# Modulation rows on three engines, and a new order of the work ahead of the first scan, in a Mamba-style block with adaptive layer norm

## The reference

```python
mod = (silu(c) @ wmod).reshape(1, 6, 1, -1)          # c: 1 x 1024, wmod: 1024 x 6144
sa, ca, ga, sb, cb, gb = (mod[:, k] for k in range(6))
ga = (2 * (ga >= 0) - 1) * maximum(abs(ga), 0.25)     # gb alike
h = layernorm(x) * (1 + ca) + sa
x = x + ga * attn(h)
h = layernorm(x) * (1 + cb) + sb
x = x + gb * ffn(h)

def attn(x):                                          # state of 16 per channel
    xp = x @ x_proj_w.T                               # 32 of dt, 16 of B, 16 of C
    dt = softplus(xp[:, :32] @ dt_proj_w.T + dt_proj_b)
    h_t = exp(dt * A) * h_(t-1) + dt * B_t * x_t      # A = -exp(A_log), a scan over the tokens
    y_t = sum over states of h_t * C_t, + D * x_t

def ffn(x):                                           # 1024 -> 2752 -> 1024, each weight with a rank-16 addition
    return down(silu(gate(x)) * up(x))
```

## Time and profile before

| | us |
|---|---|
| median of three runs | 2287.67 (2287.53 to 2288.17) |
| the profiled execution | 2279.5 |
| its span, first to last instruction | 2277.7 |
| busy in the span: TensorE matmul / VectorE / ScalarE / GpSimd | 2044.7 / 1442.4 / 1041.2 / 1542.8 |

### The profile page before, as it was taken

One profiled execution on the slowest core, in us unless ns is written; L12 is line 12 of the kernel. 1 busy time (PEld: TensorE's weight loads), 2 busy tenths in 40 slices (PEclk: granted clock), 3 DMA queues, 4 the chain that ended last, 5 costly groups with the idle time before them and its releaser, 6 DMA issues.

```text
span 2277.7 us, 33011 instructions
## 1 busy us (share of the span) xinstructions
PE 2044.7 (90%) x11652; PEld 1860.5 (82%) x11652; DVE 1442.4 (63%) x2119; ACT 1041.2 (46%) x2330; POOL 1542.8 (68%) x960
## 2 busy tenths in 40 slices
PE   7587756878879989899999899999899999999999
PEld 4233235778869989799999799999799999999999
DVE  4665776778767878767778667778667774211111
ACT  3776765666554555444545344555343332210000
POOL 1578779998988877877867777867869895110100
PEclk9688877989989999999999999999999999999999
DMA  9799875778967768586768586768587877787786
GB/s 361 301 359 342 309 289 211 279 266 277 340 248 277 255 241 283 207 274 219 246 225 280 178 280 224 242 224 284 171 268 257 280 258 256 253 287 275 253 291 218
DMA packets 121204, 602.99 MB, mean 265 GB/s; under 512 B 10576, under 2 KB 23120, under 8 KB 80464
## 3 DMA queue, kind: packets, MB, share of 16 engines
q1 hardware_dynamic: 121040, 600.89, 75.0%
HBM read 514.63 MB, written 86.21 MB: 264 GB/s over the span
## 4 chain that ended last, share of the span: by engine, by line
PE 55%; DVE 13%; POOL 9%; ACT 8%; issue 7%; DMA 6%; DVEq 0%; SPq 0%; ACTq 0%; POOLq 0%
PE FP L780 48%; DVE ring L1186 5%; POOL ring L1300 4%; PE FP L663 4%; POOL y L1275 2%; DVE ring L1071 2%; DMA raw<-w_gu 2%; ACT SC L851 2%; DVE FP L1161 2%; DMA wts<-w_scratch 2%; PE FP L804 1%; POOL wts L1283 1%; ACT sqb L969 1%; PE FP L741 1%; DMA w_scratch<-wts 1%
## 5 line engine op out<-in xcount | busy, mean ns | idle before, releaser
L780 PE MATMUL FP<-xhi,wts 128*128 128x368 f32 (+2 forms) x4320 | 1078.4, 326 | 62.9 <-ACT dtb L974 29.6
L780 PEld LDWEIGHTS FP<-xhi,wts 128*128 128x128 f32 x4320 | 774.1, 194 | 73.2 <-issue 61.5
L1300 POOL TENSOR_TENSOR ring<-ring,c_row 128x736 f32<-128x736 f32 (+2 forms) x336 | 575.7, 1714 | 236.0 <-ACT hst L868 235.7
L780 PE MATMUL FP<-xlo,wts 128*128 128x368 f32 (+2 forms) x2160 | 700.3, 324 | 0.0
L851 ACT ACTIVATE SC<-dtb,aneg 128x368 f32<-128x368 f32 (+2 forms) x768 | 409.4, 538 | 592.9 <-DVE ring L1186 592.6
L780 PE MATMUL FP<-hhi,wts 128*128 128x368 f32 (+5 forms) x2376 | 571.1, 321 | 27.6 <-POOL hlo L1315 23.2
L1186 DVE TENSOR_TENSOR_SCAN ring<-SC,hst,ring 128x368 f32<-128x368 f32 (+1 forms) x640 | 579.3, 946 | 3.6 <-ACT SC L851 3.6
L1275 POOL TENSOR_TENSOR y<-y,ring 128x736 f32<-128x736 f32 (+1 forms) x320 | 554.7, 1733 | 13.9
L780 PEld LDWEIGHTS FP<-hhi,wts 128*128 128x128 f32 (+1 forms) x2376 | 406.7, 185 | 34.9 <-POOL hlo L1315 22.3
L780 PEld LDWEIGHTS FP<-xlo,wts 128*128 128x128 f32 x2160 | 418.8, 194 | 1.1
L780 PE MATMUL FP<-hlo,wts 128*128 128x368 f32 (+5 forms) x1188 | 379.4, 319 | 0.0
(11 more groups left out here) (104 smaller groups left out, 1929.7 us busy)
## 6 DMA issues: line engine op xcount, KB each, us to landing
wts<-w_scratch SPq DMA_DIRECT2D x249, 1152.0 KB, 5.3
wts<-w_scratch SPq DMA_DIRECT2D x91, 896.0 KB, 5.0
wts<-w_scratch SPq DMA_DIRECT2D x51, 1024.0 KB, 5.5
w_scratch<-wts SPq DMA_DIRECT2D x44, 1152.0 KB, 8.6
raw<-w_gu SPq DMA_DIRECT2D x44, 576.0 KB, 6.8
modw<-mod_w SPq DMA_DIRECT2D x24, 1024.0 KB, 10.4
w_scratch<-wts SPq DMA_DIRECT2D x16, 896.0 KB, 6.8
w_scratch<-wts SPq DMA_DIRECT2D x9, 1024.0 KB, 7.8
```

What stands on the lines that cost most here:

```text
L780: last = mm(out, w, x, start=(start and k == 0 and e == 0), stop=(stop and k == n - 1 and e == 2))
L1300: G.tensor_tensor(buf, buf, over_pair(c_of(k)), ALU.mult).then_inc(g_hc, 1)
```

## The change

The twelve blocks ahead of the first scan are shared by three engines. VectorE makes 0, 3, 5, 9 and 10 (before: 2, 4, 6, 9 and 11), GpSimd makes 1 and 4, TensorE the other five (before seven). GpSimd's way with a block is new, the item `grow`: it multiplies the whole block of 8 x 256 in place by silu(c), repeated along the columns, and then adds halves: 4 x 256, 2 x 256, 256. The subtraction in `consts` moves from VectorE to GpSimd. Only two preps instead of four stand ahead of the first scan; the other two are added to those spread over the groups. And the whole list ahead of the first scan is in a new order, so that each engine has its parts, and SyncE its loads, in a new order too. `mrow` has two slots instead of four.

```diff
--- before.py
+++ after.py
@@ -41,9 +41,10 @@
 MOD_BLOCKS = 6 * D // MOD_COLS
 MOD_SLOTS = 5
 MOD_EACH = D // MOD_COLS
-ROW_SLOTS = 4
-BY_VECTOR = [2, 4, 6, 9, 11]
-BY_TENSOR = [b for b in range(MOD_BLOCKS) if b not in BY_VECTOR]
+ROW_SLOTS = 2
+BY_VECTOR = [0, 3, 5, 9, 10]
+BY_GPSIMD = [1, 4]
+BY_TENSOR = [b for b in range(MOD_BLOCKS) if b not in BY_VECTOR + BY_GPSIMD]
 LATES = [range(MOD_EACH * n, MOD_EACH * (n + 1)) for n in range(3)] + [range(b, b + 1) for b in range(3 * MOD_EACH, MOD_BLOCKS)]
 
 
@@ -209,7 +210,7 @@
 OTF = [u for u in range(NU) if u % 3 == 1]
 PREP = [u for u in range(NU) if u not in OTF]
 NPREP = len(PREP)
-PREP_BEFORE = 4
+PREP_BEFORE = 2
 
 
 def first_pieces():
@@ -224,15 +225,18 @@
     def vrow(b):
         return [("vrow", b)] + ([("lmod", b + MOD_SLOTS)] if b + MOD_SLOTS < 3 * MOD_EACH else [])
 
+    def grow(b):
+        return [("grow", b)] + ([("lmod", b + MOD_SLOTS)] if b + MOD_SLOTS < 3 * MOD_EACH else [])
+
     def cen(k, c):
         return [("cen", k, c, q) for q in range(PAIRS)]
 
-    out = [("sum", 0, 0), ("sum2", 0, 0)] + row(0) + [("lprep",)] + cen(0, 0) + [("rowc", 0)] + row(1) + vrow(2) + [("rowc", 1)]
-    out += prep() + [("sq", 0, 0), ("sq2", 0, 0), ("consts",), ("col", 0), ("col", 1), ("col", 2)] + row(3) + vrow(4) + [("rowc", 3)]
-    out += prep() + [("rstd", 0, 0), ("col", 3)] + row(5) + [("rowc", 5)] + vrow(6) + [("late", 0), ("col", 4), ("col", 5)] + prep()
-    out += [("norm", 0, 0, q) for q in range(PAIRS)] + row(7) + [("rowc", 7), ("col", 6), ("col", 7), ("late", 1), ("mod", 0)] + row(8)
-    out += [("aff", 0, 0, q) for q in range(PAIRS)] + [("rowc", 8)] + vrow(9) + prep() + [("col", 8), ("proj", 0), ("col", 9)] + row(10)
-    out += [("xs", 0), ("lx", 1), ("rowc", 10), ("dt", 0, 0), ("dt", 0, 1)] + vrow(11) + [("sp", 0, 0), ("col", 10), ("col", 11), ("late", 2), ("mod", 1)]
+    out = vrow(0) + grow(1) + [("sum", 0, 0), ("sum2", 0, 0)] + cen(0, 0) + row(2) + [("rowc", 2), ("sq", 0, 0), ("sq2", 0, 0), ("lprep",)]
+    out += vrow(3) + grow(4) + [("col", 0), ("col", 1), ("col", 2)] + vrow(5) + [("rstd", 0, 0), ("consts",), ("col", 3), ("late", 0)]
+    out += row(6) + [("rowc", 6)] + [("norm", 0, 0, q) for q in range(PAIRS)] + prep() + [("col", 4), ("col", 5)] + row(7) + [("rowc", 7)]
+    out += [("col", 6), ("col", 7), ("late", 1), ("mod", 0)] + prep() + [("aff", 0, 0, q) for q in range(PAIRS)] + row(8) + [("rowc", 8)] + vrow(9) + vrow(10)
+    out += [("proj", 0), ("xs", 0), ("lx", 1), ("dt", 0, 0), ("dt", 0, 1)] + row(11) + [("rowc", 11), ("sp", 0, 0)]
+    out += [("col", 8), ("col", 9), ("col", 10), ("col", 11), ("late", 2), ("mod", 1)]
     out += [("ini", 0, 0), ("soft", 0, 0), ("sp", 0, 1), ("keep", 0, 0), ("soft", 0, 1), ("keep", 0, 1), ("first",)]
     a = MOD_EACH
     at = {}
...
@@ -397,7 +402,7 @@
         a_hi, a_ts, a_th, a_hh = sem("weight_hi_ready"), sem("lora_rounded"), sem("tanh_ready"), sem("hidden_hi_ready")
 
         v_const, v_c, v_mod, v_modstep, v_late = sem("vector_const_ready"), sem("silu_c"), sem("mod_ready"), sem("mod_step"), sem("mod_cols_copied")
-        v_acc = sem("mod_row_summed")
+        v_acc, g_acc, g_const = sem("mod_row_summed"), sem("mod_row_summed_by_gpsimd"), sem("dt_weights_low")
         v_cen, v_step, v_norm = sem("centered"), sem("rstd_step"), sem("normed")
         v_xs, v_soft, v_add, v_u = sem("xs_split"), sem("factor_used"), sem("dt_ready"), sem("u_ready")
         v_dbx, v_ev = sem("dbx_ready"), sem("y_evacuated")
...
@@ -648,12 +655,16 @@
                     bank_free(pe, "col", b)
                 if b in BY_VECTOR:
                     pe.wait_ge(v_acc, ND * (BY_VECTOR.index(b) + 1))
+                elif b in BY_GPSIMD:
+                    pe.wait_ge(g_acc, 4 * (BY_GPSIMD.index(b) + 1))
                 else:
                     pe.wait_ge(a_row, BY_TENSOR.index(b) + 1)
                 for i in range(MOD_COLS // P):
                     out = FP[:, bank, at + i:at + i + 1]
                     if b in BY_VECTOR:
                         last = mm(out, macc[:, BY_VECTOR.index(b) % 2, i * P:(i + 1) * P], ones[:, 0:1], start=True, stop=True)
+                    elif b in BY_GPSIMD:
+                        last = mm(out, gacc[:, BY_GPSIMD.index(b), i * P:(i + 1) * P], ones[:, 0:1], start=True, stop=True)
                     else:
                         last = mm(out, mrow[0:1, BY_TENSOR.index(b) % ROW_SLOTS, i * P:(i + 1) * P], ones[0:1, 0:1], start=True, stop=True)
                 last.then_inc(pe_col, 1)
@@ -735,7 +746,7 @@
                     if c == 0:
                         pe.wait_ge(d_const, N_CONST)
                         pe.wait_ge(a_const, 4)
-                        pe.wait_ge(v_const, 2)
+                        pe.wait_ge(g_const, 1)
                     bank_free(pe, *p)
                     for i in range(ND):
                         last = mm(bank_of(*p), xpw[:, i, :], tile_of(hb, c, i), start=(i == 0), stop=(i == ND - 1))
@@ -1087,6 +1098,7 @@
                 dve.wait_ge(v_late, (2, 3, len(LATES))[n])
                 if n == 0:
                     then(V.tensor_scalar(mod[:, CA, :], mod[:, CA, :], 1.0, None, ALU.add))
+                    dve.wait_ge(a_const, 2)
                     V.tensor_scalar(aneg[:, :], aneg[:, :], -1.0, None, ALU.mult).then_inc(v_mod, 1)
                 elif n == 1:
                     then(away_from_zero(mod[:, GA, :]))
@@ -1100,9 +1112,6 @@
                 kind = p[0]
                 if kind == "mod":
                     mod_vectors(p[1])
-                elif kind == "consts":
-                    dve.wait_ge(a_const, 3)
-                    V.tensor_tensor(dlo[:, :], dtw, dhi[:, :].bitcast(F32), ALU.subtract).then_inc(v_const, 1)
                 elif kind == "vrow":
                     b, i = p[1], BY_VECTOR.index(p[1])
                     acc = macc[:, i % 2, :]
@@ -1276,7 +1285,23 @@
 
             def piece(p):
                 kind = p[0]
-                if kind == "prep":
+                if kind == "consts":
+                    pool.wait_ge(a_const, 3)
+                    G.tensor_tensor(dlo[:, :], dtw, dhi[:, :].bitcast(F32), ALU.subtract).then_inc(g_const, 1)
+                elif kind == "grow":
+                    b, i = p[1], BY_GPSIMD.index(p[1])
+                    w = modw[:, b % MOD_SLOTS, :, :]
+                    pool.wait_ge(d_mod[b % MOD_SLOTS], (b // MOD_SLOTS + 1) * 16)
+                    if i == 0:
+                        pool.wait_ge(v_c, 2)
+                    G.tensor_tensor(w, w, vec[:, 3, :].unsqueeze(2).to_broadcast([P, ND, MOD_COLS]), ALU.mult).then_inc(g_acc, 1)
+                    pool.wait_ge(g_acc, 4 * i + 1)
+                    G.tensor_tensor(w[:, 0:4, :], w[:, 0:4, :], w[:, 4:8, :], ALU.add).then_inc(g_acc, 1)
+                    pool.wait_ge(g_acc, 4 * i + 2)
+                    G.tensor_tensor(w[:, 0:2, :], w[:, 0:2, :], w[:, 2:4, :], ALU.add).then_inc(g_acc, 1)
+                    pool.wait_ge(g_acc, 4 * i + 3)
+                    G.tensor_tensor(gacc[:, i, :], w[:, 0, :], w[:, 1, :], ALU.add).then_inc(g_acc, 1)
+                elif kind == "prep":
                     i = p[1]
                     s, w = i % PREP_SLOTS, lo_cols(PREP[i])
                     pool.wait_ge(a_prep, i + 1)
```

More of the change, by code:

```diff
@@ L368, in build @@
             macc = sb("macc", [P, 2, MOD_COLS], to=early)
+            gacc = sb("gacc", [P, 2, MOD_COLS], to=early)
         xhi = sb("xhi", [P, ND, TM], F32R)
@@ L474, in mod_used @@
                 engine.wait_ge(v_acc, ND * (BY_VECTOR.index(b) + 1))
+            elif b in BY_GPSIMD:
+                engine.wait_ge(g_acc, 4 * (BY_GPSIMD.index(b) + 1))
             else:
```

## The result

The changed kernel takes 2293.45 us (median of 20 runs) and the kernel before 2286.82 (20 runs): the ratio is 1.003, 95% interval 1.0021 to 1.0039, or +6.6 us. The change makes the kernel slower by 0.3%. A second set of runs gave 1.0033 (1.0019 to 1.0046).

What follows compares the result with a forecast made beforehand. The chain over VectorE bounds the work ahead of the first scan; only the first pass's instant can move. A start 4.4 later plus 5 for preparations gave +9.4: 2287.67 to 2297 us, range 2280 to 2304 for 8 in 10.

Steps and rivals of the forecast that it cites:

- The sum: Whole kernel: first scan 4.4 us later plus scan stage 5 us longer, +9.4 us, median 2297; chance 0.40.
- the start's term: Ahead of the first scan: it starts at 78.8 instead of 74.42, 4.4 us later.
- the stage's: From first scan to first feed-forward pass: 284 us plus 5 for the two moved preparations.
- the first rival: Scan stage: the DMA queue sets it, so the preparations cost 9.7 us; +14 in all, 2302; chance 0.12.
- third: Rival, scan stage: the moved preparations vanish in slack, leaving +4.4 us, 2292; chance 0.13.
- fourth: Rival, ahead of the scan: GpSimd's product goes at half price, start as before, +5 us, 2293; chance 0.08.
- The exclusion: Ahead of the scan: VectorE instructions with two SBUF inputs and GpSimd's exclude each other whole; accumulations take 1 to 5 us, not 0.485.
- Second rival: Ahead of the scan: VectorE and GpSimd run beside each other, scan near 65.1, 9.3 us earlier; 2283 or 2278; chance 0.22.
- A block on GpSimd: Ahead of the scan: product 4.52 us, sums 2.35, 1.26 and 0.72, together 8.85 us a block.
- The order ahead of the scan: Row 0 ends at 21.9, row 3 at 39.1, row 6 at 43.3, projection at 58.2; softplus's product at 69.1, not 64.73.
- The preparations: Scan stage: 46 instead of 44 weight preparations cost 4 to 5.3 us more by their chain shares, taken as 5.
- The table load: Softplus ahead of the scan: its 1.28 us load disappears, counted as nothing because another wait covers it.

Runs made afterwards that it cites:

- The sum in PSUM: Changed kernel with VectorE's running sum in PSUM instead of SBUF until the last of eight steps: 2284.78 us, ratio 1.0000 to the kernel before.
- The two kernels with doubled stores and splits: Kernel before with 11 of the 44 scan-stage preparations' weight stores made twice, ratio 1.0043, or their GpSimd splits done twice, ratio 1.0049.
- the remedy: VectorE's running sum in PSUM, here put into the kernel before with its old order and shares: 2282.27 us, ratio 0.9989.

## Why the prediction was right, step by step

- **The sum.** +9.4 forecast, +6.6 measured (4.8 to 8.9). The direction and the range held, and both mechanisms were there. But the start's term was too large by 2 to 4 us and the stage's too small by 2, and part of the closeness of the sum is luck: these two errors cancel in part. There is also a slip in the chances: all of the forecast and the first rival and half of the third and fourth make 0.625, not 0.57, so the chance of slower was written too low.
- **The exclusion** stood, for a step with two SBUF inputs, as a reading of one row, `dlo`. The changed trace has it in nine places (eight ahead of 36 us, one at 48.62): seven are accumulating steps with both inputs in SBUF, two are TENSOR_SCALAR with one. The sum in PSUM removes all of them. Second rival: its first half (steps keep 0.485) is wrong. Its start, 65.1 or 9.3 us earlier than in the kernel before, was nearly right for the kernel in which the exclusion is taken away (66.47, 7.9 earlier).
- **A block on GpSimd.** 8.85 forecast, 8.1 measured: the sums at 2.40, 1.32 and 0.79 close to the line's 2.35, 1.26 and 0.72, the product 3.60 and not 4.52.
- **The order ahead of the scan.** Row 0 ended at 21.9 as forecast (21.86 for centering's start), by luck: VectorE began 0.5 us later than forecast and had three steps left, not two, when GpSimd began, while GpSimd's product was 0.9 shorter. Row 3 ended at 35.1, not 39.1, for three reasons. The two products were 0.9 shorter each. Taking turns cost GpSimd 0.08 us between two instructions, where the forecast charged it 0.5 for a step of VectorE, so block 4's product began at 22.48 and not at 24.0. And between 30.8 and 32.4 GpSimd waited for ScalarE, so that VectorE made three steps freely. Row 6 began at 36.1 instead of 39.1, and then lost most of it, as TensorE ran it at the lower clock (below): it ended at 42.3, not 43.3. Columns 4 and 5 so came 1 us earlier than forecast, the projection ended at 56.5, not 58.2, and the product of softplus began at 67.03, not 69.1.
- **The first scan**, +4.4, is the term that was mis-sized: +1.6 and +0.7 in two profiles. Even that is not shown by them. The two kernels with doubled stores and splits have the start of the kernel before, and their first scans came at 76.40 and 77.03. In the second a row met a split (seven steps in 5.83 us instead of 3.61); in the first the rows were as before, and the projection took 5.41 us instead of 3.72, at a granted clock of 0.67. So a start moves by 2 us from execution to execution. The kernel before with two preparations taken out took 2292.63, the changed kernel on the same chip 2292.85: all that is left for the new order and shares is 0.2 us, give or take the two or three us of the intervals. I put the start's share at 0 to 2 us.
- **The preparations**, +5, measured 6.9 and 7.1. The shares of the chain underestimate: they charge a preparation only with its own stretches of the chain, while the doubled splits cost 0.44 of their length against the share's 0.2. The first rival (9.7 by the queue) overestimates: the queue's price is 0.8 us a MB, though the DMA engines are 91% busy from 80 to 320 us.
- **The table load** was saved on ScalarE and bought nothing for softplus's first product, as forecast: it followed the vectors of the gate (66.83 + 0.17, then 67.03). From there to the first scan it took 9.0 us and not the 9.7 of the forecast: VectorE's second softplus product no longer waited 0.62 us for ScalarE. Whether the table load did that is not shown.
- **What the forecast missed**: that the new order itself was good. With the exclusion gone, the new order and shares start the scan 6 to 8 us earlier than the kernel before (66.47 and 68.11 against 74.42), some 2 us of which the remedy gives the old order too (72.59). The exclusion and the moved preparations hid it.

## What to carry to other kernels

Before giving GpSimd a part of VectorE's work, count the SBUF inputs of what VectorE does at that time: with two of them VectorE and GpSimd took turns here, and a long instruction on GpSimd held up a short one, with everything queued behind it. A running sum in an idle bank of PSUM took VectorE out of this for almost nothing: 0.14 us more on the first step of a block. Work that "fits anywhere" has a price that depends on the stage: here moving a preparation from ahead of the scan into it cost 3.5 us net, though no engine is full there. Two of them were nearly free ahead of the scan in the old order (0.3 us), cost 1.6 us of the start in the new order with the sum in PSUM, and 3.0 to 3.9 where a split also met a row of VectorE. Doubling a part of the work in a few places measures such a price.

## What the runs showed of the hardware

- VectorE and GpSimd alternated, instruction by instruction, while both had work queued: a held step ended 0.28 to 0.29 us after GpSimd's instruction, and GpSimd's next began 0.08 us after its last. Which accumulating steps are held depends on their SBUF inputs: the same step with one input in PSUM took 0.487 to 0.490 beside GpSimd, and 0.84 to 3.89 with both in SBUF. The eighth step, with one SBUF input and its output in SBUF, took 0.481, also at 22.63 beside GpSimd's product. TENSOR_SCALAR differs: with one SBUF input and its output in SBUF it took 2.75 and 1.98 beside GpSimd (0.35 alone), while from SBUF to PSUM it took 0.49 at 41.10 with a split from 41.08 on.
- GpSimd's product with an operand repeated along the last axis took 3.60 us for 2048 elements, 1.67 ns each after 0.18 fixed, against 2.12 for two full operands.
- TensorE stood idle from 30.6 to 35.2 in the changed kernel, and its next row took 6.2 us instead of 3.6. Granted clock in three stretches of it (columns as in the earlier trace rows):

```profile
30.00:35.00 5.00, 0.57 (x5) 0.48 (x4) 4.82 (x6) 2.47 (x4) 3.18 (x2) 0.96 0.76 315
36.00:42.00 6.00, 6.00 (x17) 1.85 (x17) 5.68 (x13) 0.00 (x0) 0.00 (x0) 0.55 1.08 374
43.00:50.00 7.00, 7.00 (x37) 3.35 (x37) 2.28 (x5) 3.62 (x7) 3.74 (x2) 1.00 0.93 312
```

0.55 is near the lower of the two levels, 1.2 GHz; full speed is 2.4 GHz. The kernel before shows the same after its wait of 3.70 us ahead of 39.20: 0.60 from 41 to 46. With the sum in PSUM a wait of 4.08 us stands ahead of row 6 at 29.69, and the row took 5.1 us (0.64 from 27 to 35). In the changed kernel TensorE's wait for a column so cost 2.6 us more behind it.
